# First expert unit ahead of the last norm, another row order in the q and k stacks, and one transfer moved in a decoder block on one core

## The reference

```python
x = _layernorm(x + _L0_attn_ref(x, ...))            # 16 heads of 16, rotary part, softmax over 1024 keys
x = _layernorm(x + _L0_xattn_ref(x, ctx, ctx, mask, ...))   # 16 heads of 16, 154 keys, masked
x = _layernorm(x + _L0_ffn_ref(x, choice_w, w1, w2))

probs = softmax(x @ choice_w.T)                     # 8 experts
G, I = top_k(swapaxes(probs, -1, -2), 256)          # each expert takes 256 of a batch's 1024 tokens
x_in = take_along_axis(x, I)
h = silu(x_in @ w1[e]); x_mlp = h @ w2[e]           # 256 -> 512 -> 256
out[b, I] += G * x_mlp
```

## Time and profile before

| what | value |
|---|---|
| median of the runs | 1686.72 us |
| lowest, highest | 1682.87, 1689.72 us |
| profiled execution | 1685.06 us, span 1683.3 us |
| mean granted clock of PE | 0.965 |
| PE busy | 1530.9 us (91%) |
| DVE busy | 1230.8 us (73%) |
| ACT busy | 864.3 us (51%) |
| POOL busy | 438.4 us (26%) |

### The profile page before, as it was taken

The page is one execution under the profiler, slowest core; times in us unless marked ns, Lnnn a source line. Parts: engine busy times, 40 slices in busy tenths (PEclk is TensorE's granted clock), DMA queues, the critical chain, the costliest instruction groups (busy, mean ns, idle before and its releaser), DMA issues. The chain is left out here.

```text
span 1683.3 us, 24438 instructions
## 1 busy us (share of the span) xinstructions
PE 1530.9 (91%) x8366; PEld 702.9 (42%) x8366; DVE 1230.8 (73%) x2543; ACT 864.3 (51%) x1626; POOL 438.4 (26%) x559
## 2 busy tenths in 40 slices
PE   7889999898999898989998989899987888999996
PEld 3322324424222244343232442423224436888875
DVE  5778854887888868978888689788885765664445
ACT  3367784343777743547777434477773341111111
POOL 6330001601300016013000160130000213666764
PEclk9799999999999999999999999999997898999998
DMA  6410000454100005541000054500000124555595
GB/s 178 120 55 1 2 30 9 145 116 126 40 2 1 30 5 147 117 126 39 2 1 30 10 155 104 149 16 2 2 1 26 52 70 129 113 113 110 105 267 142
DMA packets 110360, 121.52 MB, mean 72 GB/s; under 512 B 20700, under 2 KB 91868, under 8 KB 110236
## 3 DMA queue, kind: packets, MB, share of 16 engines
q1 hardware_dynamic: 95516, 99.74, 20.7%
q0 software_dynamic: 13728, 18.89, 6.2%
q10 hardware_dynamic: 992, 1.32, 0.2%
HBM read 68.76 MB, written 31.09 MB: 59 GB/s over the span
## 5 line engine op out<-in xcount | busy, mean ns | idle before, releaser
L1245 ACT ACTIVATE pT<-banks 128x512 f32<-128x512 f32 x1184 | 650.2, 600 | 277.4 <-PE banks L2121 156.2
L1565 DVE TENSOR_REDUCE nmf<-banks 128x1 f32<-128x1024 f32 x512 | 601.2, 1219 | 104.9 <-PE banks L2036 104.2
L2121 PE MATMUL banks<-qst,kst 99*128 99x512 bf16 x1024 | 342.8, 385 | 12.9 <-DVE nmf L1565 6.3
L2036 PE MATMUL banks<-kst,qst 96*128 96x512 bf16 x1024 | 311.1, 386 | 7.8 <-DVE nmf L1565 4.0
L2153 PE MATMUL banks<-pT,V 128*32 128x512 f32 x2048 | 274.6, 608 | 16.7 <-ACT oT L1233 12.3
L2121 PEld LDWEIGHTS banks<-qst,kst 99*128 99x128 bf16 x1024 | 95.7, 97 | 289.2 <-ACT pT L1245 185.1
L957 POOL CAST nmp<-nmf 128x16 bf16<-128x16 f32 x64 | 12.6, 197 | 727.0 <-issue 593.8
L2036 PEld LDWEIGHTS banks<-kst,qst 96*128 96x128 bf16 x1024 | 96.3, 99 | 121.5 <-DVE nmf L1565 26.5
L1415 ACT ACTIVATE kst<-banks 128x512 f32<-128x512 f32 x64 | 38.1, 598 | 206.7 <-PE banks L2481 206.7
L1011 POOL DMA_INDIRECT acc_rows<-kst,tok_s x62 | 100.1, 1614 | 41.4 <-issue 17.1
L1825 DVE TENSOR_SCALAR kst<-banks,gate 128x256 f32<-128x256 f32 x64 | 28.0, 479 | 93.1 <-PE banks L2494 93.1
(11 more groups left out here) (255 smaller groups left out, 2105.2 us busy)
## 6 DMA issues: line engine op xcount, KB each, us to landing
qst<-q_parts SPq DMA_DIRECT2D x36, 256.0 KB, 4.9
kst<-k_parts SPq DMA_DIRECT2D x36, 256.0 KB, 7.7
qst<-in_w SPq DMA_DIRECT2D x16, 512.0 KB, 5.2
qxs<-in_w SPq DMA_DIRECT2D x16, 512.0 KB, 5.4
qxs<-oT SPq DMA_DIRECT2D x48, 128.0 KB, 2.5
qst<-oT SPq DMA_DIRECT2D x48, 128.0 KB, 2.5
xb<-in_x SPq DMA_DIRECT2D x4, 1024.0 KB, 6.7
x_rows<-z SPq DMA_DIRECT2D x4, 1024.0 KB, 8.8
```

The source lines that it names most:

```text
L1245: act.activation(pT[:, n % RING_P, :], PS[:, banks[what, n], :], ACT.Exp, scale=scale).then_inc(s_ex, 1)
L1565: dve.tensor_reduce(nmf[:, m % 2, j, t:t + 1], scores.rearrange("p a n -> p (a n)"), AX.X, ALU.max, negate=True).then_inc(s_smu, 1)
L2036: ins = pe.matmul(pair[:, half, :], qst[0:KQ, h, t * P:(t + 1) * P], kst[0:KQ, h, half * N:(half + 1) * N], start=True, stop=True)
L2121: ins = pe.matmul(ps, kst[0:KM, head, kc * P:(kc + 1) * P], qst[0:KM, head, cols], start=True, stop=True)
```

## The change

Four edits. (1) PE turns unit 0 before the turn of the last heads, turns unit 1 after the last output projection and does unit 0's first product in two halves, before and between the turns of the normalised rows; DVE's two copies move along; the expert loop begins with unit 2's turn, and only then waits for the taken logits. (2) The DRAM rows of query and key parts are ordered half of the heads first: row = 128 x m + 8 x dim + i. A store of one chunk writes 64 x 2 rows, a load of one half reads 128 rows side by side. The contraction rows of batch 0's stacks follow the same order (`dims_of`). (3) In batch 0 the rows of group 1 are sent before `load_context(0)`. (4) `turn_rows` and `hidden` move up in the source, unchanged but for the halves.

```diff
+MC = 2
...
+        def dims_of(c, t):
+            return slice(c * KQ // C + t, (c + 1) * KQ // C, len(TERMS))
...
-                        sp.dma_start(stack[c * len(TERMS) + t:KQ:C * len(TERMS), late * 8:(late + 1) * 8,
-                                           half * N:(half + 1) * N],
+                        sp.dma_start(stack[dims_of(c, t), late * 8:(late + 1) * 8, half * N:(half + 1) * N],
...
-                rows = parts.rearrange("k (d c h) n -> k c d h n", c=C, h=H)
+                rows = parts.rearrange("k (m c r) n -> k c r m n", m=MC, c=C)
...
-                    src = parts[term[which], :, :].rearrange("(d i m) n -> m d i n", d=HD, m=2)[mc]
+                    src = parts[term[which], :, :].rearrange("(m d i) n -> m d i n", m=MC, d=HD)[mc]
...
             def self_attention(b):
-                for g in range(1, NG):
+                for g in range(1 if b else 2, NG):
                     load_minus_max(b, g, qst[:, g * G:(g + 1) * G, :])
...
+            load_minus_max(0, 1, qst[:, G:2 * G, :])
             load_context(0)
             self_attention(0)
...
                 heads_in_place(at, "oxT")
+                if not more:
+                    turned(0)
                 residual_sum(at, "yx", 0)
                 residual_sum(at, "yx", 1, lambda: normalise(b, 1, 0))
+                if not more:
+                    turned(1)
                 normalise(b, 1, 1)
...
-            turned(0)
-            turned(1)
             radix_begin(link_r)
...
+            def hidden(n, quarters=range(F // P)):
...
+                for f in quarters:
...
                 if more:
                     context_values(at)
+                else:
+                    turn_rows(0)
                 turn_heads(at, b, "oxT", True)
                 output(at, "oxT", "yx", w3)
                 if more:
                     pe.wait_ge(s_ne, (b + 1) * 2 * NG + 1 + START)
                     pe.wait_ge(s_smu, (b + 1) * SM_ALL + AHEAD)
-                turn_normalised(at, b, "x2T", 1, 2 if more else 4)
-                if more:
+                    turn_normalised(at, b, "x2T", 1, 2)
                     self_attention(at, b + 1, ORDER_NEXT)
                 else:
+                    turn_rows(1)
+                    hidden(0, range(F // P // 2))
+                    turn_normalised(at, b, "x2T", 1, 2)
+                    hidden(0, range(F // P // 2, F // P))
+                    turn_normalised(at, b, "x2T", 1, 4, 2)
                     logits(at)
-                    taken_upto(at, at.nth("lg") + 1)
...
-            turn_rows(0)
-            turn_rows(1)
-            hidden(0)
             for n in range(UNITS):
                 if n + 2 < UNITS:
                     turn_rows(n + 2)
+                if n == 0:
+                    at = Place(LAST_PLAN, B - 1)
+                    wait_taken(at, "D", at.nth("lg") + 1)
                 if n + 1 < LAST:
                     hidden(n + 1)
```

More of the change, by code:

```diff
@@ L1054, in load_first @@
                         if term[which] == part:
-                            pool.dma_start(stack[c * len(TERMS) + t:KQ:C * len(TERMS), 0:8, half * N:(half + 1) * N],
+                            pool.dma_start(stack[dims_of(c, t), 0:8, half * N:(half + 1) * N],
                                            first_parts[2 * j + c][0:P:2, part, :]).then_inc(s[half], 16)
@@ L1743, in route_early, with turned @@
                 routing_places(cols, done + 2)
+            def turned(n):
+                dve.wait_ge(s_gt, n + 1 + START)
+                dve.tensor_copy(xgT[n % 2].rearrange("p c j -> p (c j)"), PS[:, 0, :]).then_inc(s_te, 1)
             def rest_of_batch(b, more):
@@ L1810, in _ @@
             rest_of_batch(B - 1, False)
-            def turned(n):
-                dve.wait_ge(s_gt, n + 1 + START)
-                dve.tensor_copy(xgT[n % 2].rearrange("p c j -> p (c j)"), PS[:, 0, :]).then_inc(s_te, 1)
             def gated(n):
@@ L1968, in turn_late, with turn_normalised @@
                 ins.then_inc(s_item, 1)
-            def turn_normalised(at, b, name, n, upto=4):
-                for k in range(upto):
+            def turn_normalised(at, b, name, n, upto=4, first=0):
+                for k in range(first, upto):
                     half, chunk = divmod(k, 2)
@@ L2309, in context_part, with turn_rows @@
                     ins.then_inc(s_item, 1)
+            def turn_rows(n):
+                q, k = divmod(n, SLOTS)
+                pe.wait_ge(s_g[k], q * 32 + 32)
+                pe.wait_ge(s_te, n + START)
+                pe.wait_ge(s_cr, EARLY * TURNS + 2 + max(0, min(n - 2, TURNS + 2)))
+                for c in range(C):
+                    for j in range(2):
+                        ins = pe.transpose(PS[:, 0, c * CAP + j * P:c * CAP + (j + 1) * P],
+                                           xg[k][:, j, c * P:(c + 1) * P], ident[:, :])
+                ins.then_inc(s_gt, 1)
+            def hidden(n, quarters=range(F // P)):
+                w, k = weights_of(n), n % 2
+                pe.wait_ge(s_we[w % WEIGHTS], (w // WEIGHTS + 1) * 32)
+                pe.wait_ge(s_te, n + 1 + START)
+                if n:
+                    pe.wait_ge(s_si, (n - 1) * 2 + START)
+                for f in quarters:
+                    for c in range(C):
+                        ins = pe.matmul(PS[:, 2 + 2 * k + f // 2, (f % 2) * CAP:(f % 2 + 1) * CAP],
+                                        we1[w % WEIGHTS][:, c, f * P:(f + 1) * P], xgT[k][:, c, :],
+                                        start=(c == 0), stop=(c == C - 1))
+                    if f % 2:
+                        ins.then_inc(s_h, 1)
             def logits(at):
@@ L2457, in _ @@
             rest_of_batch(B - 1, False)
-            def turn_rows(n):
-                q, k = divmod(n, SLOTS)
-                pe.wait_ge(s_g[k], q * 32 + 32)
-                pe.wait_ge(s_te, n + START)
-                pe.wait_ge(s_cr, EARLY * TURNS + 2 + max(0, min(n - 2, TURNS + 2)))
-                for c in range(C):
-                    for j in range(2):
-                        ins = pe.transpose(PS[:, 0, c * CAP + j * P:c * CAP + (j + 1) * P],
-                                           xg[k][:, j, c * P:(c + 1) * P], ident[:, :])
-                ins.then_inc(s_gt, 1)
-            def hidden(n):
-                w, k = weights_of(n), n % 2
-                pe.wait_ge(s_we[w % WEIGHTS], (w // WEIGHTS + 1) * 32)
-                pe.wait_ge(s_te, n + 1 + START)
-                if n:
-                    pe.wait_ge(s_si, (n - 1) * 2 + START)
-                for f in range(F // P):
-                    for c in range(C):
-                        ins = pe.matmul(PS[:, 2 + 2 * k + f // 2, (f % 2) * CAP:(f % 2 + 1) * CAP],
-                                        we1[w % WEIGHTS][:, c, f * P:(f + 1) * P], xgT[k][:, c, :],
-                                        start=(c == 0), stop=(c == C - 1))
-                    if f % 2:
-                        ins.then_inc(s_h, 1)
             def expert_out(n):
```

## The result

| what | before | changed |
|---|---|---|
| median of the runs | 1686.01 us | 1667.54 us |
| lowest, highest | 1682.87, 1689.72 us | 1666.52, 1668.46 us |
| profiled execution | 1685.06 us, span 1683.3 | 1666.64 us, span 1664.8 |
| mean granted clock of PE | 0.965 | 0.968 |

The account below looks back on a forecast made before the run. PE, busy 91% of the span, was taken to bound the kernel. 1685.06 - 9.5 (A) - 6.5 (C) - 4.5 (B) = 1664.6 us; with 1.66 for the median 1666, range 1658 to 1677.

Parts of the forecast that it names:

- A: End of the last batch: first expert units' turns and products moved into PE's gaps, saving 9.5 us, ends 5.3 and 11.
- the upper end of A: End of the last batch: saving of 11 us if unit 0's turn also keeps the clock up for the 16 head turns.
- Its lower end: End of the last batch: saving of only 5.3 us (8.5 - 3.2) if PE's clock falls in spite of the filler.
- C: Batch 0's self attention: group 1's rows sent ahead of the context, saving 6.5 us, ends 4 and 6.9.
- The local sum: Batch 0's self attention: PE's wait of 4.38 us and 2.5 of half clock both go, 6.9 us.
- B: Cross attention of batches 0 to 2: new row order speeds stack stores and loads, saving 4.5 us, ends 0 and 7.
- Step (1): Parts stores write 64 x 2 rows instead of 8 x 16; loads start at most 1.7 us earlier per batch.
- Step (2): Stack loads read 16 runs of 16 KB instead of 128 of 2 KB; at 331 GB/s, 7.9 instead of 12.4 us.
- Rival 1: Stack loads no faster, perhaps because of their 16 target partitions; B only 0 to 3.4, 1667 to 1671 us; chance 0.22.
- Rival 4: Stack loads of one run served by fewer engines, 37 us longer in three batches, 1708 us; chance 0.04.
- Rival 3: Expert part does not follow its earlier start: late gathers or bounding scatters; A near 2, 1674 us; chance 0.06.

## Why the prediction was right

**A, 9.5 forecast; 11.5 in the first trace pair, 8.8 on chip one.** Each step stands as it was told, with one sign missed: PE's idle time before the last turns is 1.58 us, where none over 1 was to be left, and the clock held in spite of it. The rest is seen: the last turns and logits at full clock, the copies free, the table load and the indicators hidden, the gathers early enough. The surplus of 2.0 is what the upper end of A allowed for: the head turns (2.56 to 1.97) and the output products (8.17 to 7.15) ran at the higher clock, 1.6 together. The forecast left the output products out of that end. Its lower end does not add up as told: 1.6 for unit 1's products and about 3 for late last turns are 4.6, not the 3.2 taken off. The clock held, so that end was not reached.

**C, 6.5 forecast; 5.7 in the first pair, 5.6 over all kernels, 6.6 on chip one.** The mechanism is seen row by row, the wait of 4.38 and the half clock behind it are gone. The local sum was 6.9. The stage varies by 4 us among kernels that are alike in it, so that what lies between 5.6 and 6.9 can't be placed. The 10 us allowed for the context stores and their landing were 3.0 (94.54 to 97.56).

**B, 4.5 forecast; 5.7 in the first pair, 4.9 from the sums over the three cross attentions** (385.6 us, mean of the four profiles with the old order; 380.7, mean of nine with the new one, that of the loads side by side left out). The size is right, but in part by luck, since the split behind it was half wrong. Step (1), stores faster by at most 1.7 us a batch, holds to the tenth: 3.6 us from last store to first load became 1.8. Step (2), loads at more than 250 GB/s, failed, and so did the sign that ACT would wait under 1 us in each batch: it waits 1.1 to 1.9. The first row is a stretch of loads in the kernel before, the second one in the changed kernel:

```profile
337.00:349.00 12.00, 11.35 (x87) 3.80 (x85) 10.29 (x68) 4.95 (x10) 1.80 (x8) 1.00 1.04 228
```

```profile
330.00:341.00 11.00, 10.95 (x79) 4.50 (x80) 9.00 (x63) 6.27 (x12) 1.16 (x6) 0.91 1.04 240
```

That is 5% more, where the forecast took half of the way from 212 to 331 GB/s; the 212 was read from 345 to 352 us alone, and the longer stretch above has 228. Rival 1 had that part of the matter. Its reason, the 16 target partitions, is made likely and not shown: with other partitions the loads fell to 123 GB/s. Its price was too low, since a row transfer whose loads start 1.7 us earlier, and which lands another 0.9 us sooner after them, removes 2.6 of a wait of 3 to 6 us in each batch, and with it all of PE's 5.3. The new place of batch 0's own heads, which the forecast took at nothing, was not tried apart.

The share of the stores rose from 0.56 to 0.64 and not to near 1, as the forecast wanted. SP issues six such stores in 3.84 us, and 6 x 128 KB in that time are 205 GB/s, which is the rate seen: they go as fast as SP issues them. The rule of the Trainium skill (DMA: Bandwidth & Descriptors, section on why a DMA increments its semaphore by 16) put the stores on 16 engines. The trace agrees in that the share left 0.56. By the 512 B of the same page of the Trainium skill, Specifications, the length of a run would change nothing. The two runs with pieces of 2 KB nearly bear it out (217 and 223 GB/s against 227 to 240; 0.9 and 3.5 us of time).

**Rival 4** did not come, as loads of one run were not slower. But its price can be read off the loads side by side: it forecast 37 us in three batches for loads at half their rate, with the point of change at 148 GB/s. At 123 GB/s the three cross attentions took 417.0 - 380.6 = 36 us more than in the changed kernel on that chip, and the kernel was slower than the one before.

**Rival 3** had a small share of truth in another place: PE's gain of 20.4 us arrives with 18.5 at the end, because the last scatters keep their own time.

**What was not foreseen.** Self attention of batches 1 and 3 took 1.6 and 2.3 us more in the changed kernel's profile. Nothing of the change lies there; PE waits 1.6 for DVE at one place in both kernels, and in the changed one alone the granted clock is down behind it, the first row being the two us of the wait, the second what follows:

```profile
558.00:560.00 2.00, 0.51 (x3) 0.01 (x1) 2.00 (x3) 0.98 (x2) 0.00 (x0) 1.00 0.00 0
560.00:565.00 5.00, 4.91 (x22) 1.00 (x22) 2.16 (x9) 2.76 (x5) 1.11 (x4) 0.66 0.03 7
```

The kernel before has the same wait 8.8 us later, and the clock stays up behind it:

```profile
568.80:573.80 5.00, 4.88 (x28) 1.24 (x28) 3.25 (x13) 3.74 (x8) 1.11 (x4) 1.00 0.02 7
```

In batch 1 this goes with the edits. In all nine profiles that have both the new order and the early rows the clock falls there, and the stage is 208.5 to 208.8 us long; in the five that lack one of them it does not fall, and the stage has 206.3 to 207.2. So 1.3 to 2.5 us go with B and C together, a cost that the forecast did not have. How they bring it about was not traced. In batch 3 the stage takes 206.4 to 208.9 in no such order: the longest and the shortest are both among kernels with the new order. The 2.0 us of the last cross attention do not belong to the change: the changed kernel on chip two takes 106.9 for it, as the kernel before takes 107.0. The forecast came out so close by luck, because a surplus in A and B and these 2.0 us, which no term holds, met the loss in the self attention and the one at the scatters: 5.7 + 5.7 + 2.0 + 11.5 - 4.6 makes 20.3 at PE's last products, 18.5 at the end.

## What to carry to other kernels

Work that is ready early and lies at the start of the next phase is best put into the waits of the serial tail before it: the wait pays for it, and what follows keeps the full clock. Here unit 0's 16 product instructions cost 3.8 us in the gaps instead of 5.21, and the last turns and the logits 1.06 and 1.05 instead of 1.94 and 1.89. In a queue issued in order, look at what a short urgent transfer stands behind, in the issuing queue and in the DMA engines; here 12 KB cost a stop of PE in both places. And before giving a transfer longer runs, measure what bounds it: here the load that reads in one piece moved 5 to 7% more, and the store of another shape, which let it start 1.7 us earlier, was worth more. Last, look for the price of a change where it has no line: here a later stage, which no edit touched, ran at half clock for a while wherever two of the edits stood together.

## What the runs showed of the hardware

- Loads of 256 KB into 16 partitions: 6 apart they ran at 217 to 240 GB/s, side by side at 123. Runs of 16 KB (227 to 240) were only 5 to 7% above pieces of 2 KB at a distance of 2176 or 4096 bytes (217, 223) on the same chip.
- Writing a store's pattern with one more split of a dimension did not change the transfer: a share of 0.64 and 206 to 207 GB/s both times, where the old shape has 0.56 and 174. Whether an edit reached the hardware is read from the share and the rate, not from the source.
- The same kernel differs between chips in one place: in all eight profiles of chips one and three, and in none of the six others, ACT stood still for 5 us in the last cross attention, after PE had long written what it is said to have waited for, and PE lost 2.7 to 2.95 us. The changed kernel's profile is 1670.2 us long on chip three, against 1664.8 and 1667.5 us without the pause. What ACT waited for does not show in the trace and was not settled; single parts of the change are therefore to be compared on one chip.
- 16 turns of 128 x 128 cost 1.97 us where PE was kept busy, 2.56 in the kernel before and 3.0 to 3.6 where PE had stood still 11 to 12 us earlier, though it had worked between.
- A wait of 1.58 us for DVE in self attention stands in all 14 profiles at 172 to 173 us of batch 1's stage. Behind it the granted clock fell in nine of them (0.66 over 5 us in the changed kernel) and stayed at 1.00 in five; the stage is 1.3 to 2.5 us longer where it fell.
